# Layer 0 attention: a block's score matmuls in one row, its cross scores read by one VectorE instruction

## What is computed

```
ln_out = _ln(hidden_states, ln_w, ln_b)
q  = _ln(fp8_linear(ln_out, wq, ...).reshape(b, s, g, hpg, d), qln_w, qln_b)
k  = _ln(fp8_linear(ln_out, wk, ...).reshape(b, s, g, d), kln_w, kln_b)
v  = fp8_linear(ln_out, wv, ...)
core = _gqa(q, k, v)                 # self attention over 256 tokens
qx = _ln(fp8_linear(ln_out, wqx, ...), qxln_w, qxln_b)
kx, vx = split(einsum('bsi,oi->bso', cond, w_kv_x)); kx = _ln(kx, kxln_w, kxln_b)
xout = _gqa(qx, kx, vx)              # cross attention over 1601 context rows
cat = concatenate([core, xout]); catq = div_clamp_fp8(cat, proj_smooth)
return einsum('bsi,oi->bso', catq, wproj) * scale
# _gqa: softmax(q k^T / sqrt(128)) v, with 8 groups of 2 heads, head size 128
```

## Time and profile before

| | |
|---|---|
| median of 3 runs | 1788.65 us (1786.4 to 1791.87) |
| the profiled execution, span | 1787.7 us |
| PE busy | 1631.5 us, 91% of the span |
| DVE busy | 1474.9 us, 83% |
| ACT busy | 1386.3 us, 78% |
| POOL busy | 1367.9 us, 77% |
| attention of layer 0 | from about 60 to about 1260 us |
| mean granted clock of TensorE | 0.976 |

### The profile page before, as it was taken

One profiled execution on the slowest core, in us unless ns is written; L12 is line 12 of the kernel. 1 busy time (PEld: TensorE's weight loads), 2 busy tenths in 40 slices (PEclk: granted clock), 3 DMA queues, 4 the chain that ended last, 5 costly groups with the idle time before them and its releaser, 6 DMA issues. The chain is left out here.

```text
span 1787.7 us, 44278 instructions
## 1 busy us (share of the span) xinstructions
PE 1631.5 (91%) x16245; PEld 1038.3 (58%) x16438; DVE 1474.9 (83%) x3476; ACT 1386.3 (78%) x2365; POOL 1367.9 (77%) x1171
## 2 busy tenths in 40 slices
PE   3389999999999999999999999997898999999997
PEld 1256776777767767777777777765454333333332
DVE  8889999999999989999999999998896765645422
ACT  4287887888878777887887888775234999999996
POOL 3557787887878888888888888887897998979500
PEclk8599999999999999999999999999899999999999
DMA  4268999999899979999999999998523222222100
GB/s 168 93 130 180 184 187 193 198 194 190 189 199 184 200 150 198 191 231 184 195 195 192 217 213 190 194 186 160 171 42 110 41 44 75 43 37 43 31 14 13
DMA packets 603176, 261.42 MB, mean 146 GB/s; under 512 B 568784, under 2 KB 575952, under 8 KB 601552
## 3 DMA queue, kind: packets, MB, share of 16 engines
q1 hardware_dynamic: 602960, 258.57, 70.1%
HBM read 99.15 MB, written 17.28 MB: 65 GB/s over the span
## 5 line engine op out<-in xcount | busy, mean ns | idle before, releaser
L1800 PE MATMUL pv<-PT,VV 128*128 128x256 bf16 (+1 forms) x2880 | 340.9, 275 | 9.2 <-DMA PT<-PB 9.2
L1780 PE MATMUL score<-KK,QT 128*128 128x512 bf16 (+2 forms) x1795 | 315.6, 318 | 32.6 <-DVE mxp L1249 24.3
L2370 POOL TENSOR_TENSOR l_rr<-l_rr,mhalf 128x32 f32<-128x32 f32 (+1 forms) x60 | 332.8, 5546 | 5.0
L1521 ACT ACTIVATE PB<-S,rsum 128x1024 bf16<-128x1024 f32 (+1 forms) x256 | 246.2, 988 | 105.3 <-DVE rsum L1281 101.1
L1800 PEld LDWEIGHTS pv<-PT,VV 128*128 128x128 bf16 (+1 forms) x2880 | 280.7, 99 | 76.4 <-issue 35.2
L1272 DVE SCALAR_TENSOR_TENSOR PB<-S,rsum,PB 128x1024 bf16<-128x1024 f32 (+1 forms) x256 | 318.7, 1246 | 2.7 <-ACT PB L1521 2.6
L1780 PEld LDWEIGHTS score<-KK,QT 128*128 128x128 bf16 x1920 | 159.9, 98 | 164.5 <-DVE mxp L1249 32.3
L1511 ACT ACTIVATE S<-S,nmx 128x1601 f32<-128x1601 f32 x128 | 209.7, 1638 | 28.3 <-DVE nmx L1263 27.8
L2636 ACT ACTIVATE P<-score 128x1024 f32<-128x1024 f32 x196 | 199.4, 1063 | 12.7 <-PE score L2728 6.0
L1076 POOL TENSOR_SCALAR S<-S,rsum 128x256 f32<-128x256 f32 x128 | 122.0, 954 | 86.1 <-DVE rsum L1281 86.1
L2748 PE MATMUL pv<-P,V 128*9 128x256 f32 (+1 forms) x2288 | 153.9, 384 | 3.8 <-DVE pv L2174 2.4
(11 more groups left out here) (275 smaller groups left out, 3686.7 us busy)
## 6 DMA issues: line engine op xcount, KB each, us to landing
x<-rs_d SPq DMA_DIRECT2D x16, 936.0 KB, 7.6
rsb<-rs_d SPq DMA_DIRECT2D x16, 936.0 KB, 6.0
wsb<-w_split SPq DMA_DIRECT2D x46, 256.0 KB, 4.7
wsb<-w_split SPq DMA_DIRECT2D x23, 512.0 KB, 5.2
wpr<-in_wprojT SPq DMA_DIRECT2D x23, 512.0 KB, 3.9
context_d<-stage SPq DMA_DIRECT2D x16, 400.2 KB, 3.7
l_ctx<-context_d SPq DMA_DIRECT2D x4, 1601.0 KB, 8.1
rawh<-in_w_all SPq DMA_DIRECT2D x12, 512.0 KB, 5.6
```

What stands on the lines that cost most here:

```text
L1521: e.activation(m.PB[n % 2][:, 2 * a:a + b], m.S32[n % 2][:, a:b], ACT.Copy, scale=m.rsum[n % 2][:, 1:2]).then_inc(s["p_hi"], 1)
L1780: i = e.matmul(m.score[:, at:at + b - a], qt[:, kind, qp, q * P:(q + 1) * P], kk[:, kp, a:b], start=(k == 0), stop=(k == 2))
L1800: i = e.matmul(m.pv[:, at:at + 256], vv[0:rows, v, t, :], m.PT[k % 2][0:rows, turned(c, a), :], start=(c == first and r == 0), stop=(c == ...
L2370: e.tensor_tensor(rr, rr, m.mhalf[0:rows, 0:NH1], ALU.pow).then_inc(s["l1_rr"], 1)
```

## The change

A block's score matmuls now stand together: `scores(n)` issues all 15, and raises one count where it raised two. `scaled(n)` reads the 1601 context columns in one instruction and the 256 own columns in a second; the small tile `mxp` goes. The counts that other engines wait for are adapted (`mm` from 3 to 2 for a block, `bank_full` from 2 to 1). A block's matmuls may start only when both instructions for the block before have run, and VectorE's first read may start only when all 15 have. In the loop bodies of TensorE and VectorE the pieces are put in a new order; those of ScalarE, GpSimd and SP are as they were.

```diff
-    def scaled(n, piece):
+    def scaled(n):
...
-        if piece == 0:
-            if n % 4 == 0:
-                e.wait_ge(s[f"rs_in{it % 2}"], 16 * (it // 2 + 1))
-            if n >= 2:
-                e.wait_ge(s["s_lo"], n - 1)
-                e.wait_ge(s["p_lo"], 2 * (n - 1))
-            e.wait_ge(s["bank_full"], 2 * n + 1)
-        elif piece == 1:
-            e.wait_ge(s["bank_full"], 2 * n + 2)
-            e.wait_ge(s["mm"], 3 * n + 1)
+        if n % 4 == 0:
+            e.wait_ge(s[f"rs_in{it % 2}"], 16 * (it // 2 + 1))
+        if n >= 2:
+            e.wait_ge(s["s_lo"], n - 1)
+            e.wait_ge(s["p_lo"], 2 * (n - 1))
+        e.wait_ge(s["bank_full"], n + 1)
+        for kind, a, b, at, key in ((1, 0, SC, 0, 0), (0, SELF0, SELF0 + S, SELFC, SC)):
...
@@ dve_attention, loop body @@
-        scaled(4 * it, 0)
         p_lo(4 * it - 1, 0)
+        scaled(4 * it)
         keys_low(it + 1, 0)
...
-        scaled(4 * it, 1)
-        scaled(4 * it, 2)
+        offset(4 * it)
         p_lo(4 * it - 1, 1)
-        offset(4 * it)
         smooth(2 * it - 2)
         keys_low(it + 1, 1)
...
-        scaled(4 * it + 1, 0)
         exponents(2 * it - 2)
...
-        scaled(4 * it + 1, 1)
-        scaled(4 * it + 1, 2)
+        scaled(4 * it + 1)
         keys_low(it + 1, 2)
...
-        scaled(4 * it + 2, 0)
+        scaled(4 * it + 2)
         smooth(2 * it - 1)
         p_lo(4 * it + 1, 0)
+        offset(4 * it + 2)
         squares_out(it + 1)
...
-        scaled(4 * it + 2, 1)
-        scaled(4 * it + 2, 2)
+        p_lo(4 * it + 1, 1)
         values_low(it + 1, 1)
...
-        offset(4 * it + 2)
...
+        scaled(4 * it + 3)
         query_full(it + 1, 1)
...
-        p_lo(4 * it + 1, 1)
+        offset(4 * it + 3)
         values_low(it + 1, 2)
-        scaled(4 * it + 3, 0)
         exponents(2 * it - 1)
...
         invert(4 * it + 2)
-        scaled(4 * it + 3, 1)
-        scaled(4 * it + 3, 2)
         values_low(it + 1, 3)
...
-        offset(4 * it + 3)
@@ pe_attention, scores @@
-        if n:
-            e.wait_ge(s["mm"], 3 * (n - 1) + (1, 3)[half])
+        if n:
+            e.wait_ge(s["mm"], 2 * n)
```

48 lines of the change are left out of this document (19 added, 29 removed).

## The result

The changed kernel takes 1932.2 us (median of 4 runs, 1926.9 to 1936.1), the kernel before 1787.5 us in the same comparison (1784.0 to 1791.9): a ratio of 1.080 with an interval of 1.077 to 1.083. It is 145 us slower, where 51 us were forecast; the end of the range was 1882 us. The profiled execution has a span of 1930.2 us. The direction was right and the size was not.

The account below looks back on a forecast made before the run. TensorE was taken to bound late rounds, VectorE's score read to lengthen early ones. A 37.6 us loop adds 8, 10 and 30 us, context pieces 4, the last round wins about 1: +51 us, some 1840 us; range 1796 to 1882 us.

Parts of the forecast that it names:

- the loop: Chain over VectorE, GpSimd and ScalarE from one row statistics to the next: 37.6 us, setting the round; chance 0.55.
- (c): VectorE's read of D waits for GpSimd's split of block B's self part, behind the key norms' power: 3 us.
- Rival 1: Shorter loop, only (a) and (b) count: 36.1 to 36.9 us a round, 1793 to 1816 us; chance 0.18.
- (a): C's exponentials behind ScalarE's norms copy, then C's inverse, GpSimd's query norms 9.78 us behind it, and normalisation of 1.48 us.
- (b): Block B's second transpose, queued behind the row norms' way out and back: alone 2.75 us of wait in the round.
- Rival 2: No chain uses up its slack, TensorE runs through, early rounds fall to 34.85 us: -34 us, 1755 us; chance 0.09.
- Rival 3: TensorE's 2.3 us wait brings a half-speed clock stretch each round: +36 us on top, 1876 us; chance 0.13.
- the 48 us that the forecast had for the rounds: Rounds lengthened to 37.6 us: 8 us over early, 10 over middle and 30 over late rounds.
- a bound of 0.8 us down: GpSimd's magnitudes at 1.93 instead of 2.71 us would make the loop 36.8 us, +27 us in all.
- the 4 us for GpSimd's context pieces: Four rounds in which GpSimd also splits a context piece lengthen the loop by some 1 us each.
- the 3 us wait: VectorE's wait ahead of D's read for GpSimd's split of B, said to hide the early rounds' extra VectorE work.
- the last link: From VectorE's first queries to the next row statistics: 12.5 us, from 10.35 plus later reads of B and C.

Follow-up runs that it names:

- the two-read kernel: The changed kernel's order, but VectorE reads a block's context scores in two instructions, 1024 and 577 columns: 1942.8 us, ratio 1.087.
- The split ahead of the power: The changed kernel with GpSimd's self split of block B ahead of the power for the key norms: 1893.8 us, ratio 1.059.
- D moved alone: The kernel before with only block D read whole, its matmuls ahead of the second query transpose, its read ahead of the full-precision queries: 1886.9 us.
- D back: The changed kernel with block D's matmuls behind the last value product again and its read behind C's inverse: 1838.2 us, ratio 1.028.
- the filling: The changed kernel with unused matmuls in TensorE's idle places ahead of the projection and the first query transpose: 1923.3 us, ratio 1.076.

## Why the prediction was wrong in its size

**The bound now, and the start.** Right: TensorE in late rounds, VectorE's reads in early ones: with D's read merged in its old place the early rounds are shorter and the late ones are not. In the changed kernel the reads lie on the loop, and there less VectorE work does win.

**The instruction.** Right: 1601 columns take 1.82 us (1.81 forecast), and the two-read kernel gives 0.35 us a round for it.

**What is late next.** Right in each place: D's read waits 2.9 us for the split of B, TensorE waits 2.1 us ahead of the projection and then ahead of the first query transpose, nothing for the maximum. The split ahead of the power shows that (c) is paid, D moved alone that the loop is closed by this move. One reading was off: nine VectorE instructions stood between the statistics and D's first piece, not six. Rival 1 (only (a) and (b)) did not come true here. With D back the late round is 36.7 us, inside the 36.1 to 36.9 that the rival had, but that kernel gives TensorE 2.2 us more cover and was expected at 35.7 us, so the agreement is luck. Rival 2 had no case. Rival 3, the clock in each round at 1.2 us: the stretches did come, in 23 rounds, but most lie beside the loop; by the filling they cost 9 us in all.

**The loop's sum is the step that failed:** 37.6 us where it is 39.8 in the late rounds without a slow-clock stretch. Over 30 rounds the links differ from the forecast by 92 us, which with the 48 us that the forecast had for the rounds makes 140 of the 141 us:

| term | over 30 rounds |
|---|---|
| C's inverse to the query norms, 10.8 and 10.9 for 9.78 | +31 us |
| the full-precision queries to C's inverse, 2.29 for 1.84 | +14 us |
| norms to VectorE's first queries, 6.2 for 5.4 in late rounds | +16 us |
| D's read behind the weight split, rounds 1 to 11 | +16 us |
| first queries to the statistics, slow-clock stretches in rounds 12 to 22 | +12 us |
| D's read and the full-precision queries, 2.90 for 2.8 | +3 us |

The first three, 61 us, have in the main one cause. I took most durations from rows of the kernel before, where these instructions met no partner or another one, and they stand beside each other differently once the order is moved. For two of the three rows a run shows it. With a short partner the link to C's inverse falls to 1.34 us, so the meeting costs 0.95 us; my estimate of 0.6 us for the offset and 0.6 for the value rounding was too long by 0.5 and hid half of it. With the exponent cut's partner short the link to the first queries is 3.86 us, against 3.90 forecast. GpSimd's +31 us is read from the traces alone; no run took it away. Of GpSimd's +1.0 us, the last instruction for C's split has +0.87, the add +0.57, and the magnitudes -0.41 against the 2.71 of the earlier trace rows. The prediction had noticed such a row and gave it a bound of 0.8 us down. Upward it had only 0.5 us, for waits at the offsets; that an instruction of 0.16 us could take 1.15 and one of 0.29 us 2.10 was not looked for. About 3 of the 31 us are round 1's, whose chain took 12.5 us; that was not looked into. And of the 4 us for GpSimd's context pieces the trace has 1.3, in round 14 (3.59 us for 2.29), and nothing in rounds 19 to 21. The Trainium skill (SBUF — State Buffer, section "SBUF: two separate sides") has the shared port as a lock that one of the two holds for its whole instruction. By that rule a VectorE instruction of 0.16 us can cost 1.15 us, and the runs agree: 0.19 us when GpSimd's partner is cut to 8 columns. The same rule stood in the prediction, and I used it for the size of one row and not for every pair on the path.

**The early rounds** failed too: "the extra VectorE work of the early rounds stands in the 3 us wait" forgot that this work waits for ScalarE, which comes late. It is 16 us of the 92; moving the work won it in odd rounds and lost it in even ones.

**Whole blocks.** That B and C are read later was in the 12.5 us of the last link, and that was right (12.31). As a cost of its own I had not weighed it: in the changed kernel it stands inside the loop, 12.31 for 10.22 us with pieces, and C whole in its late place costs 48 us by itself. These are two ways to lose: in the changed kernel TensorE's matmuls are early and VectorE hardly waits for them (0.9 us in 60 reads, 0.6 in 57), but the whole read stands ahead of the statistics; in the late place it waits for them. I took the whole blocks as the harmless half of the change; with their order they are a third of the loss.

## What to carry to other kernels

When an order is moved and a chain over several engines becomes the bound, take its links at their contended length: go through the VectorE and GpSimd instructions that will now stand beside each other and give each meeting the length of the partner. A score buffer held once can live by being read in pieces: one instruction for all of it saves 0.2 us of VectorE and gives up the overlap of matmuls and read, 1.4 to 1.8 us a round where the reader comes early. Block D, whose matmuls stood in one row already, lost nothing in sum. And a wait of 3 us is cover only for work whose own inputs are there.

## What the runs showed of the chip

- A VectorE instruction on 128x2 with both inputs in SBUF took 1.15 us beside a GpSimd instruction of 1.15 us, in every round, and 0.16 to 0.19 us without it. The other way, a GpSimd copy of 0.40 us took 2.37 us beside a row of VectorE instructions.
- An instruction with one SBUF input was held as well: the 16-bit exponent cut took 2.10 us beside a GpSimd instruction of 2.17 us, and 0.29 us with that cut to 8 columns. The Trainium skill (GPSIMD Engine Reference, section "1. Specifications") names two-port modes of VectorE beside two SBUF inputs as the cases that contend; the runs show the long instruction for this form, and no trace shows the mode that it ran in.
- Idle times of TensorE of 2.0 us, twice in a round, were followed by a stretch at a granted clock of 0.50 (1.2 instead of 2.4 GHz) in most of the rounds 12 to 22 and in two of the seven behind them. One such stretch fell behind an idle time of 2.0 us ahead of a transpose (868.9 us), the round was 41.5 instead of 39.8 us for it, and filling both places with matmuls took all but one of them away.
